# Two-layer graph network: score and bias rows spread by TensorE, first loads reordered, weight parts and one adjT later

## The chip, the cores and the metric

The kernel runs on one core of one Trainium2 chip. The metric is the time of one execution on the device in microseconds (us), the median of several runs. Lower is better.

## What is computed

128 graphs of 128 nodes with 256 features pass through two residual blocks, each on a layer-normed and rectified input:

```python
h = relu(layernorm(x))                       # block 1
Xw = h @ Wv + bv;  sj = Xw @ aw[:d, 0];  si = Xw @ aw[d:, 0]
e = leaky_relu(sj[:, None, :] + si[:, :, None] + ab[0], 0.2)
T = adj * exp(e);  T = T / (T.sum(-1) + 1e-12)
x = x + relu(h @ Wk[0] + bk[0] + T @ h @ Wk[1] + bk[1] + T @ T @ h @ Wk[2] + bk[2])
h = relu(layernorm(x))                       # block 2
y = relu(adj @ (h @ W1) + b1);  y = relu(adj @ (y @ W2) + b2)
out = x + adj @ (y @ W3) + b3
```

## The kernel before

The graphs go in 64 pairs (`G = 2`). A fully unrolled loop of 67 rounds (`rounds`, L215) writes the program of every engine; in round i four pairs are in flight: pair a = i (layer norm, scores, attention), b = i - 1 (end of block 1, second layer norm, first product with adj), c = i - 2 (GCN layers 1 and 2), d = i - 3 (last product, output, store). The order on each engine is written out by hand in the function `one` of that engine, and semaphores join the engines; an engine takes its instructions strictly in that order. Most products are made of three: each operand is cut into a high part (ScalarE copies it to fp32r) and a low part (VectorE or GpSimd subtracts), and high x high, high x low and low x high are summed in PSUM. The names end in `_hi` and `_lo`.

Round 0 and the code ahead of it hold the set-up. **SP** (L276 to L294) issues the loads of x and adj blocks of the first pairs; `aw_bc`, `bv_bc`, `ab_bc` (score vector and its biases), `bk_bc` and `bias_out` are loads that read one row and write it to all 128 partitions (256, 128, 0.5, 384 and two of 128 KB). **ScalarE's** queue issues Wv and the three Wk. **VectorE** forms `wva` = Wv times each half of aw by four `dot`s (L771) and `half_c` from bv, aw and ab (`score_constant`). The score columns are two more columns of the weight `w_p2`, so that `p2_product` also gives the scores; `scores_copy` (L431) takes them as `uv`, and `spread_scores` (L871) spreads them over partitions. **GpSimd** makes the low parts of the Wk (L365 to L368), then in round 0 `sum_biases` (L370) which waits for all loads counted by `biases_in`, `adjT_low`, and `gcn_weights_low` (the low parts of W1, W2, W3). `adjT_hi`, `adjT_lo` are parts of the transposed adj that only the last product `z3_product` reads. **TensorE** has transposes of the identity that nothing reads (`keep_busy`, L1009): 19 before the first work, 18 after `turn_h` of pair 0, 19 in round 1, and some in the last rounds.

The chain of a pair through block 1: `x_statistics`, `rstd` (GpSimd), `x_norm` -> `turn_h` (transposed h in `bank_turned`) -> `hT_high`, `hT_low` -> `p2_product`, `p01_product` -> `attention` (`alpha`), `aT_high`, `aT_low` -> `ap_product` -> `y1_sum` (`y_full`), `y1_high`, `y1_low` -> `ay_product` -> `h_sum` (`hb`) -> `residual` (`x1`) -> `x1_statistics`, `rstd`, `shift`, `norm` (`h`) -> `m_product` -> `m_high`, `m_low` -> `z1_product` -> `layer_result(0)` (`y__hi`, `y_full`) -> `y_low(0)` -> `s2_product`. `p0_bias` (L694) adds the summed block-1 bias, and `out_bias` (L337) on GpSimd makes x1b = x1 + b3, which `finish` reads two rounds later.

Of the kernel before, what the change touches and what calls it, by code (L numbers as in the profile page):

```python
# [38 lines left out]
BUSY_BEFORE, BUSY_BETWEEN, BUSY_SECOND, BUSY_TAIL = 19, 18, 19, 16  # L39
# [8 lines left out]
def gnn_kernel(nc, x, adj, Wv, bv, aw, ab, Wk, bk, W1, b1, W2, b2, W3, b3, out):  # L48
    N_PAIRS = x.shape[0] // G
    ctx = ExitStack()  # L50
    with ctx:
# [25 lines left out]
        bk_bc = sb("bk_bc", [P, K, D])  # L77
# [170 lines left out]
        def _(sp):  # L248
# [35 lines left out]
            sp.dma_start(bk_bc[:], bk.rearrange("(o k) d -> o k d", o=1).to_broadcast([P, K, D]))\  # L284
              .then_inc(biases_in, 16)
            load_adj_blocks(1, 1)
            for g in range(G):
                sp.dma_start(bias_out[:, g, :], row(b3).to_broadcast([P, D])).then_inc(biases_in, 16)
# [20 lines left out]
        def _(pool):  # L309
            pool.memset(ident[:], 0.0).then_inc(ident_zero, 1)  # L310
# [69 lines left out]
            def one(i, k):  # L380
# [697 lines left out]
```

## Time and profile before

| | us |
|---|---|
| median of 3 runs (881.37 to 883.54) | 881.63 |
| the profiled execution's own time | 881.72 |
| its span, first to last instruction | 879.9 |
| PE busy in the span | 864.7 |
| VectorE busy | 760.2 |
| ScalarE busy | 628.2 |
| GpSimd busy | 435.8 |

In rows of the profile PE is TensorE, PEld its weight loads, DVE VectorE, ACT ScalarE, POOL GpSimd, SP SyncE. A row of the timeline gives start and duration, engine, line, operation, output<-inputs, count, and in brackets how long the engine was idle before it and what released it. Digits behind tile names are left out there, so `y_full` and `stats` stand for several tiles. Two engines' durations overlap freely; the time of the program is that of the chain through them.

### The profile page before, as it was taken

How to read it: one execution, taken by the hardware profiler on the slowest of the kernel's cores; microseconds unless marked ns; L12 is line 12 of the kernel's file. 1: busy time of each engine (PE TensorE's matmuls, PEld its weight loads, DVE VectorE, ACT ScalarE, POOL GpSimd, SP SyncE). 2: the span in 40 equal slices, each digit the busy share in tenths (PEclk: the TensorE clock that was granted, in tenths of full speed). 3: DMA queues.
4: the chain of work that ended last, by engine and by line, in shares of the span. 5: the costliest groups of instructions: out<-in, count | busy, mean ns of one | idle time of the engine just before them, and what ended most of it. 6: DMA issues, size and time to landing. Idle time of an engine off the chain costs nothing.

```text
span 879.9 us, 20848 instructions
## 1 busy us (share of the span) xinstructions
PE 864.7 (98%) x6480; PEld 817.7 (93%) x6480; DVE 760.2 (86%) x2001; ACT 628.2 (71%) x1543; POOL 435.8 (50%) x532
## 2 busy tenths in 40 slices
PE   8899999999999999999999999999999999999996
PEld 7799999999999999999999999999999999999996
DVE  5789889889889889889889889899889889889872
ACT  4477777777777777777777777777777777777773
POOL 4454454454454454454454454454454454454452
PEclk9899999999999999999999999999999999999999
DMA  8112122122122122122122122122122122122001
GB/s 202 36 34 57 36 61 56 36 61 56 37 61 57 35 61 56 36 61 57 36 61 58 35 61 57 35 62 56 35 61 57 35 62 57 35 61 58 18 25 37
DMA packets 107869, 46.18 MB, mean 52 GB/s; under 512 B 72560, under 2 KB 107504, under 8 KB 107760
## 3 DMA queue, kind: packets, MB, share of 16 engines
q1 hardware_dynamic: 106672, 43.81, 20.0%
q8 instruction: 53, 0.87, 0.4%
q10 hardware_dynamic: 1088, 1.05, 0.4%
q14 instruction: 56, 0.46, 0.2%
HBM read 28.05 MB, written 16.78 MB: 51 GB/s over the span
## 4 chain that ended last, share of the span: by engine, by line
PE 95%; SPq 1%; POOL 1%; ACT 1%; issue 1%; DMA 1%; DVE 0%; DVEq 0%; ACTq 0%; POOLq 0%
PE bank L856 43%; PE bank_p L856 35%; PE bank_turned L856 7%; PE bank_T L856 5%; PE bank_turned L867 3%; PE bank_T L877 2%; SPq L261 1%; DMA bias_col<-in_L_gnn_b 1%; POOL w_gcn_lo L361 0%; PE bank_p L1012 0%; POOL bias_h L377 0%; ACT h L487 0%; ACT y_full L524 0%; DVE aT_lo L573 0%; SPq L252 0%
## 5 line engine op out<-in xcount | busy, mean ns | idle before, releaser
L334 POOL TENSOR_TENSOR y__lo<-y_full,y__hi 128x256 fp32r<-128x256 f32 x256 | 190.1, 764 | 112.3 <-ACT y_full L524 112.3
L325 POOL TENSOR_TENSOR rstd<-veps,minus_half 128x2 f32<-128x2 f32 x128 | 88.9, 695 | 236.4 <-DVE veps L596 236.4
L856 PE MATMUL bank_p<-w_p_hi,h0T_hi 128*128 128x258 f32 (+1 forms) x512 | 176.3, 360 | 0.1
L856 PE MATMUL bank_p<-w_p_lo,h0T_hi 128*128 128x258 f32 (+1 forms) x512 | 165.3, 339 | 0.0
L856 PE MATMUL bank_p<-w_p_hi,h0T_lo 128*128 128x258 f32 (+1 forms) x512 | 142.1, 339 | 0.7 <-DVE h0T_lo L629 0.7
L856 PE MATMUL bank<-w_gcn_hi,y__hi 128*128 128x256 f32 x512 | 132.8, 292 | 1.5 <-ACT y__hi L524 1.3
L856 PE MATMUL bank<-w_gcn_lo,y__hi 128*128 128x256 f32 x512 | 127.8, 282 | 0.0
L524 ACT ACTIVATE y__hi<-bank,bias_col 128x256 fp32r<-128x256 f32 x256 | 119.7, 467 | 3.0 <-PE bank L856 3.0
L524 ACT ACTIVATE y_full<-bank,bias_col 128x256 f32<-128x256 f32 x256 | 121.6, 475 | 0.0
L350 POOL TENSOR_TENSOR adjT_lo<-adjT_full,adjT_hi 128x256 fp32r<-128x256 f32 x64 | 64.9, 1015 | 82.8 <-ACT adjT_hi L429 82.8
L856 PEld LDWEIGHTS bank_p<-w_p_hi,h0T_hi 128*128 128x128 f32 x512 | 97.3, 190 | 6.2 <-POOL w_p_lo L356 0.3
L856 PEld LDWEIGHTS bank_p<-w_p_lo,h0T_hi 128*128 128x128 f32 x512 | 97.1, 190 | 5.5
L856 PEld LDWEIGHTS bank<-w_gcn_hi,y__hi 128*128 128x128 f32 x512 | 97.4, 190 | 2.1 <-ACT y__hi L524 1.5
L856 PEld LDWEIGHTS bank<-w_gcn_lo,y__hi 128*128 128x128 f32 x512 | 97.5, 190 | 0.0
L856 PEld LDWEIGHTS bank_p<-w_p_hi,h0T_lo 128*128 128x128 f32 x512 | 83.4, 188 | 12.3 <-DVE h0T_lo L629 0.9
L344 POOL TENSOR_TENSOR x1b<-x,bias_out 128x512 f32<-128x512 f32 x64 | 82.9, 1296 | 0.0
L856 PE MATMUL bank<-w_gcn_hi,y__lo 128*128 128x256 f32 x512 | 82.2, 283 | 0.0
L487 ACT ACTIVATE h<-x,nshift,rstd 128x256 f32<-128x256 f32 x128 | 69.9, 593 | 15.5 <-DVE nshift L619 15.5
L573 DVE TENSOR_TENSOR s_lo<-bank,s_hi 128x512 fp32r<-128x512 f32 x64 | 44.3, 692 | 41.4 <-ACT s_hi L507 41.4
L453 ACT ACTIVATE z<-bank_T,uv 128x128 f32<-128x128 f32 x128 | 40.0, 364 | 55.8 <-PE bank_T L877 55.7
L507 ACT ACTIVATE s_hi<-bank 128x512 fp32r<-128x512 f32 x64 | 38.2, 597 | 53.4 <-PE bank L856 53.4
L856 PEld LDWEIGHTS bank<-adjT_full,s 128*128 128x128 f32 x512 | 66.8, 191 | 6.2 <-ACT s L501 1.1
(92 smaller groups left out, 2346.2 us busy)
## 6 DMA issues: line engine op xcount, KB each, us to landing
x_in<-in_x SPq DMA_DIRECT2D x64, 256.0 KB, 3.0
x_new<-x_out SPq DMA_DIRECT2D x64, 256.0 KB, 2.2
adj_blocks<-in_adj SPq DMA_DIRECT2D x256, 32.0 KB, 2.3
w_raw<-in_L_gnn_Wk ACTq DMA_DIRECT2D x3, 256.0 KB, 6.9
w_raw<-in_L_gnn_W SPq DMA_DIRECT2D x3, 256.0 KB, 5.5
bk_bc<-in_L_gnn_bk SPq DMA_DIRECT2D x1, 384.0 KB, 6.1
wv_raw<-in_L_gnn_Wv ACTq DMA_DIRECT2D x1, 256.0 KB, 3.8
aw_bc<-in_L_gnn_aw SPq DMA_DIRECT2D x1, 256.0 KB, 5.6
```

The costliest lines, as they stand in the source:

```text
L325: pool.tensor_tensor(rstd[n][k % 2][:], veps[n][k % 2][:], minus_half[:], ALU.pow)\
L334: pool.tensor_tensor(y[n][1][:, c], y_full[n][:, c], plain(y[n][0][:, c]), ALU.subtract)\
L344: pool.tensor_tensor(x1b[k][:], x1[k % 2][:], bias_out[:], ALU.add).then_inc(x1b_made, 1)
L350: pool.tensor_tensor(adjT[k][1][:], adjT_full[k][:], plain(adjT[k][0][:]), ALU.subtract)\
L453: last = act.activation(z[k % 2][:, g, :], spread_ps[:, g, :], ACT.Prelu, bias=uv[k % 2][:, g, 0:1], alpha=SLOPE)
L487: last = act.activation(h1[k % 2][:, g, :], x1[k % 2][:, g, :], ACT.Relu, bias=nshift[k % 2][:, g:g + 1], scale=rstd[1][k % 2][:, g:g + 1])
L507: act.activation(s3[0][:], s3_ps, ACT.Copy).then_inc(s3_hi, 1)
L524: act.activation(dst[:, c], (z1_ps, z2_ps)[n][:, c], ACT.Relu, bias=bias_col[n][:, c:c + 1]).then_inc(made, 1)
L573: dve.tensor_tensor(dst, src, plain(hi), ALU.subtract).then_inc(signal, 1)
L856: return pe.matmul(dst, stationary, moving, start=start, stop=stop, skip_group_check=True)
L867: last = pe.transpose(turned_ps[:, c, g, :], n0[k % 2][:, g, c * P:(c + 1) * P], ident[:])
L877: last = pe.transpose(spread_ps[:, g, :], uv[k % 2][:, g, 1:2].to_broadcast([P, P]), ident[:])
```

## The change

Rows of aw and bv (2 KB, 1 KB) are loaded into one partition, and a product with a column of ones, in fp32, spreads each over 128 partitions in PSUM, from where ScalarE copies them to `aw_bc` and `bv_bc`. The three rows of bk and the row of b3 are loaded the same way; one product of ones with the three rows both sums and spreads them (`bias_h`), another spreads b3 (`bias_out`). Both biases now exist once and are read for both graphs through an access pattern of step 0. `sum_biases` is gone. On SP the bias rows come before adj of pair 1, x of pair 2 before W2 and W3, W1 after adj of pair 1. GpSimd makes the low part of W1 alone in round 0, those of W2 and W3 in round 1, and adjT_low of pair 0 in round 1; `out_bias` moves from pair b to pair c. ScalarE makes the high parts of W2, W3 late in round 1, and adjT_hi of pair 0 there too. TensorE has 11, 7 and 8 `keep_busy` in place of 19 and 18; the 19 of round 1 are gone, and `p2_product` of pair 1 stands ahead of `ay_product` of pair 0. On VectorE `hT_low` of pair 1 stands ahead of `y1_low` of pair 0.

```diff
-BUSY_BEFORE, BUSY_BETWEEN, BUSY_SECOND, BUSY_TAIL = 19, 18, 19, 16
+BUSY_FIRST, BUSY_BEFORE, BUSY_BETWEEN, BUSY_TAIL = 11, 7, 8, 16
...
             load_x(0, 0)
-            sp.dma_start(aw_bc[:], aw.rearrange("(h d) o -> o h d", h=2).to_broadcast([P, 2, D]))\
-              .then_inc(score_weights_in, 16)
-            sp.dma_start(bv_bc[:], row(bv).to_broadcast([P, D])).then_inc(score_consts_in, 16)
+            sp.dma_start(aw_row[:], aw.rearrange("(o d) x -> o (d x)", o=1)).then_inc(score_rows_in, 16)
+            sp.dma_start(bv_row[:], row(bv)).then_inc(score_rows_in, 16)
             sp.dma_start(ab_bc[:], row(ab).to_broadcast([P, 1])).then_inc(score_consts_in, 16)
             load_x(1, 1)
             load_adj_blocks(0, 0)
+            sp.dma_start(bk_rows[:], bk).then_inc(bias_rows_in, 16)
+            sp.dma_start(b3_row[:], row(b3)).then_inc(bias_rows_in, 16)
+            load_adj_blocks(1, 1)
             sp.dma_start(w_raw[:, K], W1.rearrange("(c p) d -> p c d", p=P)).then_inc(gcn_weights_in[0], 16)
...
+            load_x(2, 2)
             for n, w in ((1, W2), (2, W3)):
...
 # GpSimd, one(i, k)
-                if first(i):
-                    sum_biases()
                 if c is not None:
                     y_low(1, c, k - LAG_C)
-                if b is not None:
-                    out_bias(b, (k - LAG_B) % ROUND)
-                if (n := here(i, 0)) is not None:
+                    out_bias(c, (k - LAG_C) % ROUND)
+                if first(i):
+                    gcn_weights_low((0,))
+                if second(i):
+                    gcn_weights_low((1, 2))
+                    adjT_low(0, 0)
+                if (n := here(i, 0)) is not None and not first(i):
                     adjT_low(n, k)
-                if first(i):
-                    gcn_weights_low()
...
+            def rows_copied():
+                act.wait_ge(score_rows_spread, 2)
+                act.activation(aw_bc[:].rearrange("p h d -> p (h d)"), bank_2[:], ACT.Copy).then_inc(score_rows_copied, 1)
+                act.activation(bv_bc[:], bank_T[:, 0:D], ACT.Copy).then_inc(score_rows_copied, 1)
+
+            def biases_copied():
+                act.wait_ge(bias_rows_spread, 2)
+                act.activation(bias_h[:], bank_3[:, 0:D], ACT.Copy).then_inc(bias_rows_copied, 1)
+                act.activation(bias_out[:], bank_3[:, D:2 * D], ACT.Copy).then_inc(bias_rows_copied, 1)
+
+            rows_copied()
             act.wait_ge(p2_weights_in, 16)
...
                 if first(i):
                     p01_weights_high()
+                    biases_copied()
                 if second(i):
-                    gcn_weights_high()
+                    y1_high(0, 0)
+                    gcn_weights_high((0,))
...
+                if second(i):
+                    gcn_weights_high((1,))
+                if a is not None and not first(i):
                     y1_high(a, k)
+                if second(i):
+                    gcn_weights_high((2,))
+                    adjT_high(0, 0)
+                if a is not None and not first(i):
                     adjT_high(a, k)
...
                 y1_sum(0, 0)
+                hT_low(1, 1)
                 y1_low(0, 0)
...
             pe.wait_ge(ident_made, 1)
+            keep_busy(BUSY_FIRST)
+            pe.wait_ge(row_ones_made, 1)
+            pe.wait_ge(score_rows_in, 16 * 2)
+            matmul(bank_2[:], ones[0:1, :], aw_row[:], True, True).then_inc(score_rows_spread, 1)
+            matmul(bank_T[:, 0:D], ones[0:1, :], bv_row[:], True, True).then_inc(score_rows_spread, 1)
             keep_busy(BUSY_BEFORE)
...
                 if second(i):
-                    keep_busy(BUSY_SECOND)
+                    p2_product(a, k)
...
+                if first(i):
+                    pe.wait_ge(bias_rows_in, 16 * 2)
+                    matmul(bank_3[:, 0:D], ones[:], bk_rows[:], True, True).then_inc(bias_rows_spread, 1)
+                    matmul(bank_3[:, D:2 * D], ones[0:1, :], b3_row[:], True, True).then_inc(bias_rows_spread, 1)
```

The start of TensorE's program (`bank<-ident` or `bank_p<-ident` is `keep_busy`), before:

```order
L849 UNCONDITIONAL_BRANCH
L1012 MATMUL bank<-ident 128x128 x19
L867 MATMUL bank_turned<-ident,n_0 128x128 x4
L1012 MATMUL bank<-ident 128x128 x18
L856 MATMUL bank_p<-w_p_hi,h0T_hi 128x258
```

and with the change:

```order
L1035 MATMUL bank_p<-ident 128x128 x11
L875 MATMUL bank<-aw_row,ones 128x512
L875 MATMUL bank_T<-bv_row,ones 128x256
L1035 MATMUL bank_p<-ident 128x128 x7
L886 MATMUL bank_turned<-ident,n_0 128x128 x4
L1035 MATMUL bank_p<-ident 128x128 x8
L875 MATMUL bank_p<-w_p_hi,h0T_hi 128x258
```

Two products stand in the queue between the first and the second group of unread transposes, and behind a wait for two loads. Further on, between `p2_product` and `spread_scores` of pair 0, stand the two bias products:

```order
L875 MATMUL bank_p<-w_p_lo,h0T_hi 128x258
L875 MATMUL bank_p<-w_p_hi,h0T_lo 128x258 x4
L875 MATMUL bank<-bk_rows,ones 128x256
L875 MATMUL bank<-b_row,ones 128x256
L898 MATMUL bank_T<-ident,uv 128x128 x2
```

TensorE at the turn from round 0 to round 1, before and with the change (`n_1` is pair 1's normed input, `y_0` pair 0's y1):

```order
L867 MATMUL bank_turned<-ident,n_1 128x128 x4
L1012 MATMUL bank<-ident 128x128 x19
L856 MATMUL bank_T<-y_0_hi,aT_hi 128x256
L856 MATMUL bank_T<-y_0_lo,aT_hi 128x256
L856 MATMUL bank_T<-y_0_hi,aT_lo 128x256
```

```order
L886 MATMUL bank_turned<-ident,n_1 128x128 x4
L875 MATMUL bank_p<-w_p_hi,h0T_hi 128x258
L875 MATMUL bank_p<-w_p_lo,h0T_hi 128x258
...
L875 MATMUL bank_p<-w_p_hi,h0T_lo 128x258 x4
L875 MATMUL bank_T<-y_0_hi,aT_hi 128x256
L875 MATMUL bank_T<-y_0_lo,aT_hi 128x256
L875 MATMUL bank_T<-y_0_hi,aT_lo 128x256
```

The 19 transposes are gone, and pair 1's first product stands where they stood, ahead of pair 0's `ay_product` (`bank_T<-y_0`). GpSimd after the weight parts of the Wk, before and with the change:

```order
L325 TENSOR_TENSOR rstd_1<-veps_1,minus_half 128x2
L373 TENSOR_TENSOR bias_part<-bk_bc 128x256
L377 TENSOR_TENSOR bias_h<-bias_part,bk_bc 128x256 x2
L350 TENSOR_TENSOR adjT_lo<-adjT_full,adjT_hi 128x256
L361 TENSOR_TENSOR w_gcn_lo<-w_raw,w_gcn_hi 128x512 x3
L325 TENSOR_TENSOR rstd_0<-veps_0,minus_half 128x2 x2
L344 TENSOR_TENSOR x1b<-x_0,bias_out 128x512
L350 TENSOR_TENSOR adjT_lo<-adjT_full,adjT_hi 128x256
```

```order
L333 TENSOR_TENSOR rstd_1<-veps_1,minus_half 128x2
L369 TENSOR_TENSOR w_gcn_lo<-w_raw,w_gcn_hi 128x512
L333 TENSOR_TENSOR rstd_0<-veps_0,minus_half 128x2 x2
L369 TENSOR_TENSOR w_gcn_lo<-w_raw,w_gcn_hi 128x512 x2
L358 TENSOR_TENSOR adjT_lo<-adjT_full,adjT_hi 128x256 x2
L342 TENSOR_TENSOR y__lo<-y_full,y__hi 128x256 x2
```

The bias sums are gone, x1b is no longer between `rstd` and `adjT_lo`, and the low parts of W2, W3 and of both pairs' adjT now stand directly ahead of pair 0's first `y__lo`.

## Rows read from the trace of the kernel before

**Rows 1.** The page, part 2: granted clock in tenths, 40 slices
```profile
PEclk9899999999999999999999999999999999999999
```

**Rows 2.** Waits of PE after 38 us: who for whom, total, times, longest
```profile
PE bank L856 <- DVE s_lo L573: 1.4, 1, 1.4
...
PE bank_p L856 <- ACT aT_hi L467: 0.2, 1, 0.2
```

**Rows 3.** Stretches: length, PE, PEld, DVE, ACT, POOL busy, clock, DMA, GB/s
```profile
31.00:38.00 7.00, 6.31 (x30) 6.02 (x31) 4.08 (x11) 1.84 (x4) 1.01 (x1) 0.52 0.00 0
```

**Rows 4.** Timeline, `spread_scores` of pair 2
```profile
41.29 0.38 PE L877 MATMUL bank_T<-ident,uv 128*128 128x128 f32 x2
```

**Rows 5.** DMA issues up to 13 us, median us to landing
```profile
aw_bc<-in_L_gnn_aw SPq DMA_DIRECT2D x1, 256.0 KB, 5.6
...
ab_bc<-in_L_gnn_ab SPq DMA_DIRECT2D x1, 0.5 KB, 7.7
```

**Rows 6.** Timeline, pair 0's way to its products: start, us, engine, operation
```profile
1.52 4.31 PE L1012 MATMUL bank<-ident 128*128 128x128 f32 x19 [1.52 <-POOL ident L316]
...
4.24 0.75 DVE L579 BATCH_NORM_STATS2 stats<-x_in 128x6 f32<-128x256 f32 x2 [4.24 <-DMA x_in<-in_x]
...
7.03 0.42 DVE L750 CUSTOM_DVE_ANT_0 scratch<-wv_raw,aw_bc 128x256 f32<-128x256 f32 x1
...
7.50 0.63 ACT L410 ACTIVATE w_p_hi<-w_raw 128x512 fp32r<-128x512 f32 x1 [3.40 <-DMA w_raw<-in_L_gnn_Wk]
...
8.08 3.46 PE L1012 MATMUL bank<-ident 128*128 128x128 f32 x18
...
11.30 0.36 PE L856 MATMUL bank_p<-w_p_hi,h0T_hi 128*128 128x258 f32 x1
...
13.03 0.26 ACT L439 ACTIVATE uv<-bank_p,half_c 128x4 f32<-128x4 f32 x1 [1.28 <-PE bank_p L856]
...
13.35 0.43 PE L877 MATMUL bank_T<-ident,uv 128*128 128x128 f32 x2 [0.35 <-ACT uv L439]
...
13.89 0.51 PE L856 MATMUL bank_p<-w_p_hi,h0T_hi 128*128 128x512 f32 x1
```

**Rows 7.** Timeline, one fp32 product of four matmuls at the full clock
```profile
46.33 1.05 PE L856 MATMUL bank_turned<-adjT_full,h 128*128 128x128 f32 x8
```

**Rows 8.** Timeline, aT_lo of pair 0, then from y1 of pair 0 to its h
```profile
16.32 0.43 DVE L573 TENSOR_TENSOR aT_lo<-alpha,aT_hi 128x256 fp32r<-128x256 f32 x1 [0.54 <-ACT aT_hi L467]
...
17.94 2.24 PE L1012 MATMUL bank<-ident 128*128 128x128 f32 x19
...
18.08 0.88 DVE L683 SCALAR_TENSOR_TENSOR y_full<-bank_p,rinv,p 128x256 f32<-128x256 f32 x2
...
21.21 0.69 DVE L701 TENSOR_TENSOR p0b<-bank_p,bias_h 128x512 f32<-128x512 f32 x1 [0.70 <-POOL bias_h L377]
...
23.07 0.86 DVE L710 SCALAR_TENSOR_TENSOR hb<-bank_T,rinv,p0b 128x256 f32<-128x256 f32 x2
```

**Rows 9.** Timeline, low parts of W1 to W3, then pair 1's attention
```profile
21.77 4.21 POOL L361 TENSOR_TENSOR w_gcn_lo<-w_raw,w_gcn_hi 128x512 fp32r<-128x512 f32 x3
...
29.27 1.27 POOL L344 TENSOR_TENSOR x1b<-x,bias_out 128x512 f32<-128x512 f32 x1
29.31 1.51 DVE L573 TENSOR_TENSOR aT_lo<-alpha,aT_hi 128x256 fp32r<-128x256 f32 x1 [0.77 <-ACT aT_hi L467]
29.33 0.51 PE L856 MATMUL bank_p<-p_hi,aT_hi 128*128 128x258 f32 x2 [1.84 <-ACT aT_hi L467]
...
31.22 1.85 PE L856 MATMUL bank_turned<-adjT_full,h 128*128 128x128 f32 x8
...
34.61 1.01 POOL L350 TENSOR_TENSOR adjT_lo<-adjT_full,adjT_hi 128x256 fp32r<-128x256 f32 x1 [4.07 <-ACT adjT_hi L429]
```

**Rows 10.** Chain of waits, twelve matmuls twice: start, us, what
```profile
33.76 2.93 PE bank L856 x12
...
53.58 1.43 PE bank L856 x12
```

More of the change, by code:

```diff
@@ L76, in gnn_kernel @@
         ab_bc = sb("ab_bc", [P, 1])
-        bk_bc = sb("bk_bc", [P, K, D])
+        aw_row = sb("aw_row", [1, 2 * D])
+        bv_row = sb("bv_row", [1, D])
+        bk_rows = sb("bk_rows", [K, D])
+        b3_row = sb("b3_row", [1, D])
+        ones = sb("ones", [K, P])
         scratch = sb("scratch", [P, 6, D])
@@ L240, in landed, with each_graph @@
             return (i - k) * (16 // ROUND) + 16
-        BIAS_LOADS = 1 + G + 2
+        def each_graph(row):
+            return row.rearrange("p (o d) -> p o d", o=1).to_broadcast([P, G, D])
         block = ctx.enter_context(nc.Block())
@@ L282, in _ @@
             load_adj_blocks(0, 0)
+            sp.dma_start(bk_rows[:], bk).then_inc(bias_rows_in, 16)
+            sp.dma_start(b3_row[:], row(b3)).then_inc(bias_rows_in, 16)
+            load_adj_blocks(1, 1)
             sp.dma_start(w_raw[:, K], W1.rearrange("(c p) d -> p c d", p=P)).then_inc(gcn_weights_in[0], 16)
[L284 to L288, printed above, removed]
             for n, b in enumerate((b1, b2)):
                 sp.dma_start(bias_col[n][:], b.rearrange("(c p) -> p c", p=P),
-                             allow_slow_non_contiguous=True).then_inc(biases_in, 16)
+                             allow_slow_non_contiguous=True).then_inc(columns_in, 16)
+            load_x(2, 2)
             for n, w in ((1, W2), (2, W3)):
@@ L297, in one @@
                 if (n := here(i, -2)) is not None:
-                    load_x(n, (k + 2) % ROUND)
+                    if not first(i):
+                        load_x(n, (k + 2) % ROUND)
                     load_adj_blocks(n, (k + 2) % ROUND)
@@ L356, in k_weights_low, with gcn_weights_low @@
                 pool.tensor_tensor(lo, w_raw[:, n], plain(hi), ALU.subtract).then_inc(signal, 1)
-            def gcn_weights_low():
-                for n in range(K):
+            def gcn_weights_low(layers):
+                for n in layers:
                     pool.wait_ge(gcn_weights_hi, n + 1)
@@ L368, in _ @@
                 k_weights_low(2 + n, n, w_p01[0][:, :, cols], w_p01[1][:, :, cols], p01_weights_cut)
-            def sum_biases():
-                pool.wait_ge(biases_in, 16 * BIAS_LOADS)
-                pool.tensor_tensor(bias_part[:], bk_bc[:, 0, :], bk_bc[:, 1, :], ALU.add)\
-                    .then_inc(bias_h_made, 1)
-                pool.wait_ge(bias_h_made, 1)
-                for g in range(G):
-                    pool.tensor_tensor(bias_h[:, g, :], bias_part[:], bk_bc[:, 2, :], ALU.add)\
-                        .then_inc(bias_h_made, 1)
             def one(i, k):
@@ L507, in s3_high, with gcn_weights_high @@
                 act.activation(s3[0][:], s3_ps, ACT.Copy).then_inc(s3_hi, 1)
-            def gcn_weights_high():
-                for n in range(K):
+            def gcn_weights_high(layers):
+                for n in layers:
                     act.wait_ge(gcn_weights_in[n], 16)
@@ L769, in _ @@
             x_norm(0, 0)
-            dve.wait_ge(score_weights_in, 16 * 2)
+            dve.wait_ge(score_weights_in, 16)
+            dve.wait_ge(score_rows_copied, 2)
             for c in range(C):
@@ L805, in one @@
                     s3_low(d)
-                if a is not None:
+                if a is not None and not second(i):
                     hT_low(a, k)
@@ L1029, in one @@
                     ay_product(b, kb)
-                if a is not None:
+                if a is not None and not second(i):
                     p2_product(a, k)
```

32 lines of the change are left out of this document (19 added, 13 removed).

## The prediction

> **What bounds the kernel now.** I read the page first: PE is busy for 864.7 of 879.9 us, and the granted clock is full but for one slice near the start, from 22 to 44 us [rows 1]. Next the waits of PE after 38 us: only some 4 us in five waits, all but 0.2 us of it in the last rounds [rows 2]. So from round 2 on PE works without a stop, every round costs the sum of its products, and the change adds and removes no product there. It can only move the point at which this unbroken stretch begins. Then the windows: from 31 to 38 us PE has a granted clock of 0.52, so it ran there at the lower of its levels, 1.2 GHz, in place of 2.4 [rows 3]. All the rest is read in the timeline of the first 42 us. The landmark of the sum is `spread_scores` of pair 2, at 41.29 us [rows 4]; behind it PE has no wait but the 0.2 us.
>
> **Step 1: the front.** Before, the loads that write one row to 128 partitions land 5.6 and 7.7 us after issue [rows 5], and x of pair 0 is there at 4.24 us [rows 6]. The rows of aw and bv are issued behind that x, at the old places of `aw_bc` and `bv_bc` (the load of 0.5 KB took 7.7 us, queued behind both). No row shows a one-partition load. Bounds: with x at 4.24, or with the 7.7 us of `ab_bc`, at 9.4. I take 4.3, since nothing but x stands ahead of them now.
>
> The Trainium skill, "DMA: Bandwidth & Descriptors", section "Latency and other measured facts", gives tiny transfers about 0.8 us as a floor; by it the rows would be there before the 11 transposes end, and the sum below would gain another 0.3 us. The 0.5 KB load at 7.7 us speaks for the queue instead.
>
> Products: four fp32 matmuls of 128 columns take 0.8 us at the full clock (0.2 each; 1.05 with the drain) [rows 7]. The transposes show which clock the front has: 19 in 4.31 us at the start, 0.23 each [rows 6], against 19 in 2.24 us in round 1, 0.12 each [rows 8]. The front is at half speed (though the clock row shows nothing of it [rows 1]). So aw (512 columns) costs 1.6 us and bv 0.8: they end at 6.7. ScalarE copies both in about 1.1 us (0.63 for 512 columns [rows 6]), to 7.8. The first `dot` comes at 7.8 in place of 7.03, the high part of Wk[2] at 7.8 in place of 7.50. PE: 7 transposes to 8.3, `turn_h` 0.9, 8 transposes 1.8: `p2_product` at 11.0, before 11.30, where it waited for the end of the 18 transposes and not for its weights. A gain of 0.3 that the sum gives back at once: behind `p2_product` stand the two bias products of 256 columns, 0.8 us at the full clock, and ScalarE copies both (0.4 each) ahead of `scores_copy`. Before, `p2_product` took from 11.30 to 13.03 with its drain. Now it is done at 12.7, the bias products at 13.4, the copies at 14.2, so `uv` starts at 14.2 in place of 13.03. `spread_scores` follows 0.32 us later, `p01_product` 0.2 after that, 14.7 in place of 13.89, where it had waited for GpSimd's weight parts. **Front: 0.8 us later.** Bounds: 0 (the full clock comes early, all products halve) to 1.2 (b3's row, issued near 8 us, lands 5.6 us later, at 13.6, when the queue needs it at 12.7). I take 0.7.
>
> **Step 2: round 1 up to h.** Before, VectorE went from y1 of pair 0 (18.08, ready at 18.96) to `hb` at 23.07: 4.1 us [rows 8]. In it were 0.70 us until the bias sum came from GpSimd, a wait of the same length for the high part of y1, and five instructions. With the change the bias stands ready, and `hT_low` of pair 1 fills the wait for y1's high part, since `turn_h` and ScalarE's copy of pair 1 are done by then. What is left is `hT_low`, `y1_low`, `p0_bias` and the statistics of pair 2, about 0.69 each: 2.75. **Gain 1.35.** The 19 transposes cost nothing before (PE waited behind them for `y1_low`), and give nothing now. `p2_product` of pair 1 takes their place and is done at about 20.8, ready long before VectorE is. It no longer matters.
>
> **Step 3: attention of pair 1.** `aT_lo` took 1.51 us, from 29.31, while GpSimd's x1b ran from 29.27 for 1.27 [rows 9]; that of pair 0 took 0.43 with nothing beside it [rows 8]. x1b is moved a round later, to where its pair's x1 is long made. `aT_lo` ended at 30.82, and PE's last two attention products waited for it. All six take 0.8 in one piece from 29.33, to 30.1; `m_product` could start there in place of 31.22. **Gain 1.1**, and 0.15 from `residual`, which no longer runs beside GpSimd's W2 and W3 parts. `m_product` of pair 0 so starts 2.6 us earlier, less step 1.
>
> **Step 4: m to the scores of pair 2.** Before 31.22 to 41.29, 10.1 us. Most of it was at half clock: twelve matmuls of 256 columns took 2.93 us at 33.76 and 1.43 at 53.58 [rows 10]; `m_product`, z1, `turn_h` and `ay` together cost 3.4 us over the full clock. At full clock the waits come out: m 0.8, ScalarE's copy 0.7, z1's high part 1.0, a wait of 0.5 for `m_low`, z1's rest 0.4, `turn_h` 0.4, `ay` 0.9 with its wait, 0.2 for `hT_high` (ScalarE now has W2's, W3's and pair 0's adj parts ahead of it, 1.6 us), `p2` 1.5, s2's high part 0.9, 0.7 for `y_low`, s2's rest 0.5: 8.5. The `y_low` wait is what the change itself adds. GpSimd had two of three parts of 4.21 us (21.77 on) early; now W2, W3, adjT 0 and adjT 1 (1.27, 1.27, 1.01, 1.01) [rows 9] stand directly ahead of pair 0's `y_low`. **Gain 1.6.** Bounds: 0 if the clock falls again, 2.3 without the GpSimd queue.
>
> Against this step speaks the Trainium skill, "SBUF — State Buffer", section "Who interferes with whom": a VectorE instruction with two SBUF inputs and a GpSimd one that reads SBUF block each other in turn. This is what `aT_lo` shows, and by it the moved parts may do to `y1_low` and `residual` of pair 1 what x1b did; the sum would then be 1.1 us worse, the price of `aT_lo` once.
>
> **Sum.** 1.35 + 1.1 + 0.15 + 1.6 + 0.15 (most of PE's 0.2 in round 2) = 4.35, less 0.7: 3.6 us. Loads of W and x have slack: 1 MB less is moved. The tail's x1b of the last pair comes while its last layer is at work. Both cost 0. The profiled execution had 881.72 us, 0.09 above the median. So 881.7 - 3.6 = 878.1; I say **878.2**.
>
> **Rivals.**
> - **The clock falls again.** It fell about 31.3 us, after PE had waited 1.84 and 0.80 us with 0.7 of work between [rows 9]. The second gap goes, but the first becomes 2.2 (round 1 is paced by VectorE still), and the transposes of round 1 are gone, so gaps of about 1 us come ahead of it. Then step 4 gives nothing and the queues on GpSimd are hidden: gain 2.7 - 0.7 = 2.0, **879.7**. Beside it: the Trainium skill, "TensorE: Matmul & The Clock Gate", section "HAM oscillation", blames long single waits; by that the clock would stay up.
> - **GpSimd's queue becomes the wait.** If the four parts are blocked by VectorE's two-input work, or come late because ScalarE's high parts do, s2's rest waits 1.2 us more: **879.4**. For it: they stand in a row, and ScalarE makes W3's only after y1. Against: 64 pairs show adjT_lo at 1.01 us.
> - **The score rows come late: slower.** PE, ScalarE and VectorE all stand in order behind them. If they land at 9.4 as by `ab_bc`'s 7.7 us, the `dot`s start at 12.9; with 1.7 for them and the two small instructions behind, `p2_product` starts at 14.6, 3.3 late, and `p01_product`, with the bias products and copies, 4.3. PE idles for 5 us ahead of it, the clock stays down, and steps 2 to 4 give 2.7: 881.7 + 4.3 - 2.7, **883.3.** With the clock down it decides from rows landing some 2.3 us late, at 6.6.
> - **The change doesn't do what it says:** the blocking is moved, not removed. W1's low part (1.27) now meets `y1_low` of pair 0, at 1.2, and step 3 gives 0.2 in place of 1.1: 3.6 - 1.2 - 0.9, 1.5 gained, **880.2**.
>
> **How the numbers follow.** What this kernel's measurement can tell from no change is 0.3%, 2.6 us; faster by that is below 879.0. Forecast 0.50 (its own range 877.0 to 879.0), clock 0.22, GpSimd 0.13, score rows 0.07, ineffective 0.08. Of the forecast nearly all is below 879.0, of clock and GpSimd together a quarter: faster 0.57. Slower by over 2.6 us needs the rows later still: 0.04. Same: 0.39. The range: below, a front at no cost and no GpSimd wait, 881.7 - 5.0 = 876.7; above, up to the ineffective case and a little of the front's bound, 881.0.
>
> **What would show it.** Right: `p2_product` of pair 0 near 11.0, `uv` near 14.2, `hb` near 22.4, `aT_lo` of pair 1 at 0.43, `m_product` near 29.3, granted clock 1.00 from 31 to 38, `spread_scores` of pair 2 near 37.8, the round at the same 13.2 us. Wrong: PE's wait for a row load over 1 us, a clock of 0.5 after 28 us, `y__lo` of pair 0 behind adjT_lo by more than 1 us, or any new wait of PE after round 3.

## The result, and the profile after

| | before | changed |
|---|---|---|
| median, us | 881.94 (881.37 to 884.11, 17 runs) | 881.07 (879.08 to 881.72, 16 runs) |
| ratio, 95% interval | | 0.9983 [0.9975, 0.999] |
| the profiled execution, its span | 881.72, 879.9 | 879.17, 877.4 |

One changed execution of 1708.92 us, far outside the rest, is left out here, as are three below (936.29, 1905.07 and 2176.69 us). The gain is 0.9 us where 3.5 was forecast: within 0.3%, and just above the top of the range (881.0).

The times of the changed kernel are two groups, by the mean granted clock of each run: four runs at 879.1 to 879.2 with 0.999, twelve at 881.0 to 881.7 with 0.994 to 0.997. The kernel before has them too: in the later comparisons 879.0 to 880.1 in 12 of its 112 runs (0.996 to 0.999), and 880.7 to 884.2 in the rest. In 43 of the 112 the mean clock was 0.992 or 0.993 (median 883.0); none of the 27 timed runs of the changed kernel, later ones included, was that low. The profile below is of the upper clock, that of [rows 3] of the lower. **At the upper clock (0.998 or more) the two kernels are 0 to 0.3 us apart.** The two profiled executions differ by 2.6 us and the medians by 0.9, so the profiles flatter the change by 1.7 us, and the experiments have to take the clock apart from the rest.

The windows of the changed kernel (columns as in [rows 3]) show the full clock where the kernel before had 0.52:

```profile
31.00:38.00 7.00, 6.01 (x48) 5.45 (x46) 6.77 (x13) 5.57 (x13) 5.21 (x5) 1.00 0.00 0
```

The timeline of its front, against [rows 6]:

```profile
4.29 0.75 DVE L596 BATCH_NORM_STATS2 stats<-x_in 128x6 f32<-128x256 f32 x2 [4.29 <-DMA x_in<-in_x]
5.08 2.04 PE L875 MATMUL bank<-aw_row,ones 1*128 1x512 f32 x2 [0.82 <-DMA bv_row<-in_L_gnn_bv]
6.92 1.06 PE L875 MATMUL bank_T<-bv_row,ones 1*128 1x256 f32 x2
8.01 0.60 ACT L409 ACTIVATE aw_bc<-bank 128x512 f32<-128x512 f32 x1 [3.89 <-PE bank_T L875]
9.04 0.42 DVE L767 CUSTOM_DVE_ANT_0 scratch<-wv_raw,aw_bc 128x256 f32<-128x256 f32 x1 [1.88 <-ACT bv_bc L410]
9.48 1.37 POOL L364 TENSOR_TENSOR w_p_lo<-w_raw,w_p_hi 128x512 fp32r<-128x512 f32 x1 [3.08 <-ACT w_p_hi L419]
9.74 1.40 DVE L767 CUSTOM_DVE_ANT_0 scratch<-wv_raw,aw_bc 128x256 f32<-128x256 f32 x1
11.74 2.72 POOL L364 TENSOR_TENSOR w_p_lo<-w_raw,w_p_hi 128x512 fp32r<-128x512 f32 x2 [0.89 <-ACT w_p_hi L424]
12.04 0.36 PE L875 MATMUL bank_p<-w_p_hi,h0T_hi 128*128 128x258 f32 x1 [0.20 <-DVE w_p_lo L590]
12.41 0.92 DVE L767 CUSTOM_DVE_ANT_0 scratch<-bv_bc,aw_bc 128x256 f32<-128x256 f32 x1
13.26 1.49 DVE L767 CUSTOM_DVE_ANT_0 scratch<-bv_bc,aw_bc 128x256 f32<-128x256 f32 x1
15.18 0.15 DVE L780 TENSOR_SCALAR half_c<-c_sum 128x1 f32<-128x1 f32 x1
15.43 0.26 ACT L448 ACTIVATE uv<-bank_p,half_c 128x4 f32<-128x4 f32 x1
15.75 0.43 PE L898 MATMUL bank_T<-ident,uv 128*128 128x128 f32 x2 [0.97 <-ACT uv L448]
```

The rows landed 0.8 us behind x, the two products, at half speed, took 2.9 us, and three of six `dot`s took 0.92 to 1.49 us in place of 0.42: those that ran beside GpSimd's `w_p_lo`. `half_c` came at 15.18 and `uv` right behind it, 2.4 us later than before.

The timeline of rounds 1 and 2, against [rows 8, 9]:

```profile
20.10 0.88 DVE L700 SCALAR_TENSOR_TENSOR y_full<-bank_p,rinv,p 128x256 f32<-128x256 f32 x2
23.57 0.88 DVE L727 SCALAR_TENSOR_TENSOR hb<-bank_T,rinv,p0b 128x256 f32<-128x256 f32 x2
29.65 0.43 DVE L590 TENSOR_TENSOR aT_lo<-alpha,aT_hi 128x256 fp32r<-128x256 f32 x1 [0.77 <-ACT aT_hi L476]
29.67 0.51 PE L875 MATMUL bank_p<-p_hi,aT_hi 128*128 128x258 f32 x2 [1.91 <-ACT aT_hi L476]
30.51 1.05 PE L875 MATMUL bank_turned<-adjT_full,h 128*128 128x128 f32 x8
32.79 3.00 POOL L369 TENSOR_TENSOR w_gcn_lo<-w_raw,w_gcn_hi 128x512 fp32r<-128x512 f32 x2 [3.14 <-ACT w_gcn_hi L521]
33.27 1.37 DVE L590 TENSOR_TENSOR y_lo<-y_full,y_hi 128x512 fp32r<-128x512 f32 x1 [0.16 <-ACT y_hi L488]
35.74 1.43 POOL L358 TENSOR_TENSOR adjT_lo<-adjT_full,adjT_hi 128x256 fp32r<-128x256 f32 x2
37.14 1.86 POOL L342 TENSOR_TENSOR y__lo<-y_full,y__hi 128x256 fp32r<-128x256 f32 x2
39.63 0.38 PE L898 MATMUL bank_T<-ident,uv 128*128 128x128 f32 x2
```

From y1 to hb 3.47 us (before 4.99), from hb to `m_product` 6.94 (8.15), from there (30.51) to `spread_scores` of pair 2 9.12 (10.07). The landmark so came 1.7 us earlier, and the end of the program 2.5: another 0.4 us was gained in the very next round (13.1 us to the scores of pair 3, before 13.6), the rest in small pieces later. The view of PE's waits behind 38 us has a new one, in place of the 0.2 of [rows 2]:

```profile
PE bank L875 <- POOL y__lo L342: 1.0, 1, 1.0
```

### The profile page after: what moved, and what is told of

Its sections match the earlier page's. It is cut to its first block, busy times and chain, and to the rows that moved or that the text cites. A ratio compares the mean times of both kernels' runs of the same rounds, so it can differ in the third digit from the quotient of the medians.

```text
span 877.4 us, 20808 instructions
## 1 busy us (share of the span) xinstructions
PE 861.0 (98%) x6458; PEld 812.2 (93%) x6458; DVE 761.1 (87%) x2001; ACT 629.4 (72%) x1547; POOL 433.5 (49%) x530
## 4 chain that ended last, share of the span: by engine, by line
PE 96%; ACT 1%; POOL 1%; DVE 1%; issue 1%; DMA 0%; SPq 0%; DVEq 0%; POOLq 0%
PE bank L875 43%; PE bank_p L875 36%; PE bank_turned L875 7%; PE bank_T L875 5%; PE bank_turned L886 3%; PE bank_T L898 2%; POOL w_gcn_lo L369 0%; DMA bv_row<-in_L_gnn_bv 0%; PE bank_p L1035 0%; DVE scratch L767 0%; POOL y__lo L342 0%; POOL rstd L333 0%; POOL adjT_lo L358 0%; ACT y_full L533 0%; ACT h L496 0%
```

## Experiments

Three explanations stood against each other. **Front:** the score rows and the slowed `dot`s eat the gain. **GpSimd:** the moved low parts block `y_lo` of pair 1 and delay `y__lo`. **Clock:** the gain of step 4 was the clock's, and it falls in most runs with the change as well. Fastest runs are given beside the medians, since they stand for the upper clock; those of the changed kernel are 879.1 here and 879.3 when it was timed again, so 0.2 to 0.4 us between jobs means nothing.

### One edit alone, and repairs made singly

The kernel before with x1b alone moved (GpSimd, `one`):

```diff
                     y_low(1, c, k - LAG_C)
-                if b is not None:
-                    out_bias(b, (k - LAG_B) % ROUND)
+                    out_bias(c, (k - LAG_C) % ROUND)
```

> The kernel before with one edit: x1b is made for pair c in place of pair b. Theory A (step 3 holds: blocking of aT_lo by GpSimd's x1b cost 1.1 us on PE's path): aT_lo of pair 1 takes 0.43 in place of 1.51, m_product of pair 0 starts 0.7 to 1.1 us earlier (30.1 to 30.5 in place of 31.2), and the median falls by 0.5 to 1.5 us. Rival (the blocking only moves): aT_lo stays over 1 us or another VectorE instruction of round 1 grows by 1 us; no change of the median within 0.3 us.

Measured: 878.49 (877.68 to 880.68), ratio 0.9967 [0.9956, 0.9978]. `aT_lo` takes 0.43 and `m_product` starts at 30.59. One moved instruction gains more than the whole change; the rest of the change must cost. Six of its twelve runs are at 877.7 to 878.0. The median fell by 3.3 us where 0.5 to 1.5 was expected, so more than the moved block is in it.

The changed kernel with the bias products behind `turn_h` of pair 1, and ScalarE's copies behind y1:

```diff
                 if second(i):
+                    pe.wait_ge(bias_rows_in, 16 * 2)
+                    matmul(bank_3[:, 0:D], ones[:], bk_rows[:], True, True).then_inc(bias_rows_spread, 1)
+                    matmul(bank_3[:, D:2 * D], ones[0:1, :], b3_row[:], True, True).then_inc(bias_rows_spread, 1)
                     p2_product(a, k)
...
```

> The changed kernel with the two bias products moved from between p2_product and spread_scores of pair 0 to behind turn_h of pair 1, where PE waited 0.70 us, and ScalarE's two copies to behind y1_high of pair 0. Theory F (the front's price is mostly these: in the changed kernel p2_product began at 12.04 and uv at 15.43, 3.4 us, where before it took 1.7): uv of pair 0 comes 1.0 to 1.6 us earlier, at 13.8 to 14.4, and so does all behind it; median 1.0 to 1.6 us below the changed kernel. Rival G (half_c, late because its dots are blocked by GpSimd's low parts, holds uv at 15.3 by itself): uv at 15.2 to 15.4 and no gain above 0.2 us.

Measured: 880.61 (879.19 to 881.07), ratio 0.9981. `uv` is at 15.58, right behind `half_c` at 15.32: in the queue of PE and ScalarE the bias products were in nobody's way. The fastest runs are those of the changed kernel, 879.2.

The changed kernel with 16 unread transposes where PE waits for `aT_hi` of pair 1:

```diff
                     p01_product(a, k, 1, (1,))
+                    if second(i):
+                        pe.wait_ge(bias_rows_copied, 2)
+                        keep_busy(16, bank_3[:, 0:P])
                     ap_product(a, k)
```

> The changed kernel with 16 unread transposes (1.7 us at the full clock) in PE's wait of 1.9 us ahead of ap_product of pair 1. Theory C (the two groups of times of the changed kernel, near 879.1 and 881.1, differ by whether TensorE's granted clock falls near 30 us behind that wait): nearly all runs near 879.1 to 879.4, granted clock of the program 0.999 in all of them, median 1.5 to 2 us below the changed kernel's. Rival (the groups come from elsewhere, the loads or the front): the two groups stay, median within 0.4 us of the changed kernel's or slightly later, since the transposes may hold ap_product by 0.1 us.

Measured: 879.14 (878.93 to 881.43), ratio 0.9975. Seven of eleven runs at 878.9 to 879.2, four at 880.7 to 881.4 with a clock of 0.996 to 0.997. The wait for `aT_hi` shrinks from 1.91 to 0.16. More runs keep the clock, but not all.

The changed kernel with GpSimd's part of W3 and both adjT_lo behind `y_low(0)` of round 2:

```diff
+                if i == 2:
+                    gcn_weights_low((2,))
+                    adjT_low(0, 0)
+                    adjT_low(1, 1)
...
-                    gcn_weights_low((1, 2))
-                    adjT_low(0, 0)
...
+                    gcn_weights_low((1,))
```

> The changed kernel with GpSimd's low part of W3 and both adjT_low moved behind y_low and the two rstd of round 2. Theory Q (GpSimd's queue holds the second half of s2_product by 0.98 us): y__lo of pair 0 is done by 37.2 in place of 39.0, PE's wait of 0.98 goes, spread_scores of pair 2 at 38.6 to 38.8 in place of 39.63, and the median falls by 0.6 to 1.0 us. Rival (the wait only moves: s3_product or z3_product now wait for the late parts, or rstd of pair 1 for them): PE waits 0.5 us or more in round 2 or 3 elsewhere, median within 0.3 us of the changed kernel's.

Measured: 880.29 (879.71 to 882.03), ratio 0.9987; its fastest runs 0.6 above the changed kernel's. `spread_scores` of pair 2 came at 38.44, 1.2 us earlier, but PE then waited 1.6 us for `y__lo` behind it: the queue is as long, only its place differs.

### The front

The second experiment's edit, and the score rows by the old loads to all partitions:

```diff
-            sp.dma_start(aw_row[:], aw.rearrange("(o d) x -> o (d x)", o=1)).then_inc(score_rows_in, 16)
-            sp.dma_start(bv_row[:], row(bv)).then_inc(score_rows_in, 16)
+            sp.dma_start(aw_bc[:], aw.rearrange("(h d) o -> o h d", h=2).to_broadcast([P, 2, D]))\
+              .then_inc(score_rows_in, 16)
+            sp.dma_start(bv_bc[:], row(bv).to_broadcast([P, D])).then_inc(score_consts_in, 16)
...
```

> The changed kernel with the score rows loaded by the broadcasts of before (11 and 8, then 18 transposes, as before) and the bias products behind turn_h of pair 1. Theory D (the front's 2 us come from the score rows' way over PE and ScalarE: it puts VectorE's six dots beside GpSimd's low parts of the Wk, which block them): the dots take 0.42 each again and start near 7.0, uv of pair 0 is at 12.9 to 13.2 in place of 15.4, y_full of pair 0 near 18.1 in place of 20.1, hb near 21.6, and the fastest runs (clock 0.999) come to 877.0 to 877.6, 1.6 to 2.1 us below the changed kernel's 879.1. Rival (the front is off the path, since round 1 has slack on VectorE): fastest runs within 0.5 us of 879.1.

Measured: 879.88 (878.83 to 880.21), ratio 0.9966 [0.9952, 0.9979]. `uv` at 12.36, but `p01_product` only at 14.56: it waited 1.47 us for `w_p_lo`, and that for Wk, whose three loads took 7.3 us to land, in place of 6.0 in the changed kernel. And in this profile the clock fell in the front, 0.69 from 16 to 20 us. The fastest run, 878.83, is within the rival's 0.5 us of 879.1: of the 2 us next to nothing is regained by this alone.

```profile
14.56 0.50 PE L875 MATMUL bank_p<-w_p_hi,h0T_hi 128*128 128x512 f32 x1 [1.47 <-POOL w_p_lo L365]
```

The changed kernel with the `dot`s reading the score vector in PSUM, where the product left it, and the bias products later:

```diff
-                    dot(wva[:, c, h:h + 1], wv_raw[:, c, :], aw_bc[:, h, :], 2 * c + h, wva_made)
+                    dot(wva[:, c, h:h + 1], wv_raw[:, c, :], bank_2[:, h * D:(h + 1) * D], 2 * c + h, wva_made)
...
```

> The changed kernel with the dots reading the spread aw straight from PSUM (no copy of aw by ScalarE; bv is still copied), so that a dot has one input in SBUF at most besides bv's, and with the bias products behind turn_h of pair 1. Theory D: all six dots take about 0.42 although GpSimd's low parts run beside them, half_c is there before 13.5 in place of 15.3, uv of pair 0 at 13.5 to 13.9, and the fastest runs come to 877.4 to 878.0. Rival (the dots are slow for another reason than two inputs in SBUF beside GpSimd): some dots still take 0.9 to 1.5 us, uv stays at 15 or later.

Measured: 880.07 (879.45 to 880.87), ratio 0.9971 [0.9962, 0.9979], six runs at 879.5 to 879.6 and six at 880.6 to 880.9. VectorE's timeline:

```profile
11.83 0.41 DVE L766 CUSTOM_DVE_ANT_0 scratch<-bv_bc,bank 128x256 f32<-128x256 f32 x1
12.16 0.42 DVE L766 CUSTOM_DVE_ANT_0 scratch<-bv_bc,bank 128x256 f32<-128x256 f32 x1
12.62 0.46 DVE L776 TENSOR_TENSOR c_sum<-bva 128x1 f32<-128x1 f32 x1
13.12 1.21 DVE L778 TENSOR_TENSOR c_sum<-c_sum,ab_bc 128x1 f32<-128x1 f32 x1
14.36 0.15 DVE L780 TENSOR_SCALAR half_c<-c_sum 128x1 f32<-128x1 f32 x1
```

The `dot`s are free of GpSimd now. But the block goes to the next VectorE instruction with two inputs in SBUF, a sum of one element per partition: 1.21 us, for 0.16 in the changed kernel. So `uv` comes 0.8 us earlier, at 14.61, and not the 2.5 that the three `dot`s had lost. Nor does the 0.8 show in the time: the fastest runs are no faster than the changed kernel's 879.1, where 877.4 to 878.0 was expected.

### The weight parts, and the clock in the front

The changed kernel with the parts of W2 and W3 at their old places on ScalarE and GpSimd:

```diff
-                    gcn_weights_low((0,))
+                    gcn_weights_low((0, 1, 2))
...
-                    gcn_weights_high((0,))
+                    gcn_weights_high((0, 1, 2))
```

> The changed kernel with both parts of W2 and W3 made where they were before (ScalarE at the start of round 1, GpSimd at the end of round 0); adjT of pair 0 stays late. Theory W (moving these parts costs 0.98 us of PE's wait for y__lo of pair 0 and makes y1_low of pair 1 1.37 us long in place of 0.68): y_lo of pair 1 takes 0.68, PE waits under 0.3 us for y__lo in round 2, spread_scores of pair 2 at 38.3 to 38.8 in place of 39.63, fastest runs 878.1 to 878.5. Rival (the same work in front of uv of pair 1 and beside residual delays round 1 by as much): hb and x1 of pair 0 0.5 us later, fastest runs within 0.3 us of 879.1.

Measured: 880.92 (879.01 to 882.78), ratio 0.9974 [0.9962, 0.9986]. `y_lo` of pair 1 takes 0.69 again, but the clock is at 0.5 just there, and the median tells nothing of it. The fastest runs, 879.0 to 879.1, are the changed kernel's, as the rival said. So each of the three repairs (`dot`s, bias products, W parts) gains nothing that shows by itself.

x1b moved, and the 16 transposes, on the kernel before:

> The kernel before with x1b for pair c and 16 unread transposes ahead of ap_product of pair 1. Theory C (the clock falls behind PE's wait of 1.9 us there and costs 0.2 to 3 us, differently from run to run): runs lie within 0.6 us of one another, all with clock 0.998 or more, median 877.2 to 877.9 against 878.5 for the same kernel without them. Rival: the spread from 877.7 to 880.7 stays, because the clock falls for another wait (in the front or round 1's start).

Measured: 879.42 (878.45 to 880.42), ratio 0.9964 [0.9949, 0.9978]. In the profile the clock is full from 24 to 50 us, and fell in the front, where PE had waited 0.80 and 1.47 us:

```profile
12.00:16.00 4.00, 1.92 (x7) 1.44 (x8) 2.35 (x8) 2.08 (x6) 3.15 (x3) 0.92 0.70 131
16.00:20.00 4.00, 4.00 (x17) 3.32 (x16) 1.18 (x4) 1.08 (x3) 1.51 (x3) 0.65 0.85 222
```

There are two places to lose the clock, and a cover at one leaves the other. The front of this kernel is that of the kernel before, so the place in the front was there before the change.

### Four kernels side by side

x1b moved, and of the change only the reorder of round 1:

```diff
+                hT_low(1, 1)
                 y1_low(0, 0)
...
-                    keep_busy(BUSY_SECOND)
+                    p2_product(a, k)
```

> The kernel before with x1b moved, and with the reorder of round 1 alone: hT_low of pair 1 ahead of y1_low, p2_product of pair 1 in place of the 19 transposes; loads, bias sum and weight parts as before. Theory (the reorder is a gain of its own, and the rest of the change gives it back): hb of pair 0 some 0.7 us earlier than 23.1, since the sum of biases on GpSimd still ends at 21.2; fastest runs near 877.0, median about 0.7 below that of x1b moved alone. Rival (the reorder takes PE's cover away and the clock falls more often): fastest runs the same 877.7 or lower, but median at or above that of x1b moved alone.

The changed kernel again:

> The changed kernel again, beside the others on one chip. If the earlier runs are typical: a quarter of the runs near 879.1 with clock 0.999, the rest near 881.2; median 0.8 us below the kernel before. If the chip made the difference, the median is 3 us below.

On the changed kernel four repairs at once: `dot`s from PSUM, bias products later, W parts at their old places, 16 transposes:

> The whole change with four repairs: dots read the score rows in PSUM, bias products behind turn_h of pair 1, parts of W2 and W3 at their old places, 16 unread transposes ahead of ap_product of pair 1. If the losses are the ones named (front held by half_c and slow dots 0.8 us, y_low and y__lo blocked 0.7 us, clock), they add: uv at 14.6, y_low of pair 1 at 0.69 us, no wait for y__lo, clock full, median 877.5. Rival (each only moves the wait, as when they were made alone): median 879.5 or more, no better than x1b moved alone.

x1b moved alone, again:

> The kernel before with x1b moved and nothing else, again, on the chip of the other three. If one move is worth more than the whole change: median 2 to 3 us below that of the changed kernel in this job, fastest runs 877.7 against 879.1. If the earlier difference was chance of the clock: medians within 0.8 us of each other.

| | median | runs | ratio to before (882.1) |
|---|---|---|---|
| x1b and reorder | 879.99 | 879.66 to 882.93, 11 | 0.9984 [0.9973, 0.9994] |
| changed | 880.36 | 879.27 to 881.88, 11 | 0.9981 [0.9971, 0.999] |
| repaired | 878.44 | 878.24 to 878.52, 5 | 0.9956 [0.9944, 0.9969] |
| x1b alone | 879.33 | 878.08 to 880.79, 7 | 0.9971 [0.9957, 0.9985] |

The reorder alone is a loss, not 0.7 us of gain: its fastest runs are 1.6 us above those of x1b alone. Its profile has the lower clock in three stretches (0.63 from 16 to 20 us, 0.57 from 22 to 26, 0.58 from 32 to 36), so its times can't be split, but it shows what the expectation forgot: GpSimd's W parts start at 23.22, right when `y1_low`, now behind `hT_low`, does:

```profile
23.22 4.20 POOL L359 TENSOR_TENSOR w_gcn_lo<-w_raw,w_gcn_hi 128x512 fp32r<-128x512 f32 x3 [0.28 <-ACT w_gcn_hi L509]
23.27 1.78 DVE L570 TENSOR_TENSOR y_lo<-y_full,y_hi 128x512 fp32r<-128x512 f32 x1
```

x1b alone is again ahead of the changed kernel, by 1.0 us and not the 2 to 3 expected. The changed kernel need not lose the clock near 31 us as in [rows 3]: in the profiled run of this job (mean clock 0.996) it falls in the front, behind PE's wait of 0.90 us for `uv`, and `m_product` starts at 32.30 in place of 30.51:

```profile
12.00:16.00 4.00, 3.10 (x19) 2.39 (x17) 3.90 (x11) 1.19 (x5) 2.55 (x2) 0.99 1.05 278
16.00:20.00 4.00, 4.00 (x12) 3.25 (x13) 1.90 (x8) 2.12 (x6) 0.69 (x1) 0.58 0.21 36
```

The repaired kernel is 0.9 us above the 877.5 expected, but faster than with any one of its repairs. It has `half_c` at 14.22, `y_lo` of pair 1 at 0.69, and the landmark where the prediction had put it, 37.8:

```profile
32.90 0.69 DVE L585 TENSOR_TENSOR y_lo<-y_full,y_hi 128x512 fp32r<-128x512 f32 x1
35.52 1.47 POOL L342 TENSOR_TENSOR y__lo<-y_full,y__hi 128x256 fp32r<-128x256 f32 x2 [0.64 <-ACT y_full L531]
37.82 0.38 PE L894 MATMUL bank_T<-ident,uv 128*128 128x128 f32 x2
```

### Taking the repairs apart

> The repaired kernel without the 16 unread transposes in the gap ahead of ap_product of pair 1. If the clock is most of what is missing: its fastest runs are at 878.2 to 878.5 as those of the repaired kernel, but half or more of its runs lie 1.5 to 2.5 us above, at a mean clock of 0.997 or lower, median 879.5 or more. If the parts and the front did it: all runs at 878.5, as with the transposes.

> The repaired kernel again: dots in PSUM, bias products later, parts of W2 and W3 early, 16 transposes in the gap. If the cover holds the clock: no run above 879.0, median 878.4. If the first five runs were luck: a third or more near 880.5.

> The repaired kernel but with the parts of W2 and W3 where the change put them. If GpSimd's queue costs 0.7 to 1.0 us (y_low of pair 1 at 1.37, y__lo at 1.86 and waited for): median 879.2, spread_scores of pair 2 near 38.7 in place of 37.8. If it is hidden: 878.4.

The fourth leaves the score rows to the old loads, and covers the wait behind them:

```diff
                     spread_scores(a, k)
+                    if first(i):
+                        keep_busy(10, bank_3[:, 0:P])
```

> The repaired kernel with the score rows by the old loads to all partitions, and 10 more unread transposes behind spread_scores of pair 0, where PE waits 1.5 us for GpSimd's low parts. If spreading by TensorE is worth less than it costs (uv at 12.4, p01_product held to 14.6 by the late Wk loads, against 15.2): median 877.9, 0.5 below the repaired kernel. Rival (the loads of 384 KB push Wk back and the low parts come later still): 878.8 or more.

| | median | runs | mean clock of the runs |
|---|---|---|---|
| repaired | 878.35 | 878.23 to 878.38, 5 | 0.999 to 1.0 |
| without the 16 transposes | 879.75 | 878.24 to 880.92, 8 | 0.999 in three, 0.995 to 0.997 in five |
| W2, W3 parts late | 879.15 | 878.8 to 879.2, 5 | 0.998 to 1.0 |
| score rows by loads, both covers | 877.59 | 877.28 to 877.69, 5 | 0.999 to 1.0 |

All four medians as the first theory of each said, to within 0.3 us. No profile shows where the third had its landmark, expected near 38.7. **The clock:** without the cover the fastest runs are the same 878.2, five of eight lie 1.5 to 2.7 us above, and in the profile, behind a wait of PE of 2.25 us, the granted clock is 0.50 from 32 to 36 us, the lower level, 1.2 GHz. A matmul of 256 columns follows the last at 0.21 us there, and not at 0.12:

```profile
29.50 0.50 PE L871 MATMUL bank_p<-p_hi,aT_hi 128*128 128x258 f32 x2 [2.25 <-ACT aT_hi L474]
...
32.97 0.41 PE L871 MATMUL bank<-m_hi,w_gcn_lo 128*128 128x256 f32 x1
33.18 0.41 PE L871 MATMUL bank<-m_hi,w_gcn_hi 128*128 128x256 f32 x1
```

**GpSimd:** 0.8 us. **Score rows by TensorE** cost 0.8 us against the loads they replace (the second cover came with them, but both kernels had the full clock in all runs); the last is the fastest kernel of the study, 0.9951 [0.9939, 0.9963] of the kernel before, 4.3 us.

Last, how much of that belongs to the change at all. The kernel before with x1b moved and both covers, and with the covers alone:

> The kernel before with x1b moved, 16 unread transposes ahead of ap_product of pair 1 and 10 behind spread_scores of pair 0. If the clock is the main cost and x1b the main edit: all runs within 0.5 us of each other, median 878.0, so that the bias rows, the reorder and the loads are worth 0.4 us together (877.6 with them). If the rest of the change is worth its step 2: 878.9 or more.

> The kernel before with the two covers and nothing of the change. If the clock alone accounts for the gap between its runs of 879.3 and of 882: all runs at 879.0 to 879.5, median 879.3, 2.6 us below the kernel before. If x1b's collision is what lets the clock fall (PE waits for aT_lo behind the first wait): half the runs still at 881 or more.

Measured beside a kernel before of 882.22: 878.00 (877.91 to 879.46, 7 runs), ratio 0.9955 [0.9939, 0.9971], and 879.25 (878.91 to 879.7, 11 runs), ratio 0.9971 [0.996, 0.9982]. 26 instructions that compute nothing gain 3.0 us; x1b adds 1.25; all the rest of the change, in its best form, 0.4 (from two jobs, so not resolved).

One thing here is not the clock's. The profiled execution of the first of the two is its slowest run, 879.46 with the clock at 0.999, 1.1 us above the next. In it Wk landed a little earlier, GpSimd began 0.1 us ahead of VectorE's two one-element sums, and these took 1.17 and 1.19 us:

```profile
11.26 2.49 POOL L354 TENSOR_TENSOR w_p_lo<-w_raw,w_p_hi 128x512 fp32r<-128x512 f32 x2 [1.90 <-ACT w_p_hi L412]
11.37 1.17 DVE L756 TENSOR_TENSOR c_sum<-bva 128x1 f32<-128x1 f32 x1
12.58 1.19 DVE L758 TENSOR_TENSOR c_sum<-c_sum,ab_bc 128x1 f32<-128x1 f32 x1
14.05 0.26 ACT L436 ACTIVATE uv<-bank_p,half_c 128x4 f32<-128x4 f32 x1 [2.35 <-DVE half_c L760]
```

In the profile of the kernel before, the second sum began at 11.27 and GpSimd at 11.30, and both sums took 0.16. So the landing of Wk is a second thing that differs from run to run; in how many runs it costs time isn't known.

## Why the prediction was wrong

**Bound: right; landmark: right to about 1 us.** The round is 13.2 us in both. But from the landmark to the end it is 838.6 us before and 837.8 with the change (837.5 to 839.6 over the other profiled runs), where the sum had put 0.15 for all that lies behind it.

**Step 1, the front: mis-sized, 2.0 us where 0.7 was put (0.8 worked out, bound 1.2).** The profiled run's `y_full` came 2.0 us later. The rows landed at 5.08 and not 4.3 (0.8). The products took 2.9 and not 2.4, with a drain each. And the term that the sum left out: it priced the `dot`s at the 0.42 of [rows 6], a `dot` with GpSimd idle beside it, and moved them into GpSimd's `w_p_lo` without a price. `half_c` became the last input of `uv`; the bias products, on which the sum spent 1.6 us, cost nothing, as the second experiment shows.

**Step 2: right**, 1.52 for 1.35, but not for the order alone. Done by itself, with the bias sum and the W parts left as they were, the reorder was a loss.

**Step 3: right**, 1.2 for 1.25, and the run with x1b alone shows it to be the one edit that pays: 1.25 us with the clock held.

**Step 4: this is where it failed.** The 1.6 us were the price of the clock in a single profiled run of before (2.3, less 0.7 for GpSimd's queue), and were booked as a gain of the change, with "the clock falls again" as a rival of 0.22. In truth the clock differs from run to run in both kernels: up in 12 of 112 runs before, in 4 of 16 and 5 of 11 runs with the change. Nothing the change does covers PE's wait of 1.9 us, and the front is a second place to lose it, in both kernels. The changed kernel's median so stands 2.0 us above its own upper group. In the run where the clock stayed up, step 4 gave 0.95 and not 1.6: it took 9.1 us where 8.5 was summed, because the moved W2 and W3 parts blocked `y_lo` (1.37 for 0.69) and `y__lo` (1.86 for 1.47), so that PE waited 0.3 us for the one and 1.0 for the other, where the sum had 0.7 for the second alone. The prediction did weigh the first of them with a rule, the Trainium skill, "SBUF — State Buffer", section "Who interferes with whom", and left it out of the sum; the trace agrees with the rule, there and at the `dot`s. The repaired kernel shows both costs by their absence: its step 4 is 7.6 us.

**Sum at equal clock:** 1.5 + 1.2 - 2.0, less the 1.5 by which step 4 is longer than the repaired kernel's, is -0.8 at the landmark. This is an estimate, since no profile shows the kernel before at the full clock through step 4; with x1b moved and the clock held its step 4 is 7.6 us too. The 0.8 behind the landmark brings it to 0, and the times say 0 to 0.3 us gained. Either way there is nothing left of 3.6. The 0.9 us of the medians are that, and a better chance of the clock.

**Rivals.** The true case was three of them at once: the clock (2 us in most runs), GpSimd's queue (0.8), and a bit of the late rows (0.8 of the front). Each was priced alone, the first two at 879.7 and 879.4, both far from 881.1; the third, with rows 5 us late, at 883.3, but they were 0.8 us late. What stays open: what decides in which runs the clock falls, since the same waits stand in profiles with and without a fall.

## What to carry to other kernels

When a profile shows a stretch at the lower clock, ask first in how many runs it does: a mean clock beside each time tells most of it (not all, as the slow run at 0.999 shows), and one profile can flatter a change by 2 us of 880. If the time is lost there, cover every wait ahead of the stretch with work that nobody reads, and do it before anything else is moved; it cost nothing here and was worth more than the whole change. A VectorE instruction that is moved must be priced beside what GpSimd does at its new time: in these runs one with two inputs in SBUF, even one element wide, waited GpSimd's instruction out, and an operand left in PSUM freed it only until the next such instruction. And where two repairs stand one behind the other on the way, each alone may show nothing: the three here gained only together, 1.0 us between the fastest runs of one job (878.2 against 879.3).

## What the runs showed of the hardware

- A sum of one element per partition took 1.21 us beside GpSimd's `w_p_lo`, and 0.16 without. Two inputs in SBUF are not needed for it: a copy of four elements per partition, with one input, took 1.02 us beside `w_p_lo` in the kernel before, and 0.17 with GpSimd idle in the changed kernel.

```profile
8.53 1.02 DVE L775 CAST w_p_hi<-wva 128x4 fp32r<-128x4 f32 x1
```

- The clock fell in the front of the changed kernel (0.58 from 16 to 20 us) behind a wait of 0.90 us, the longest since PE's first instruction 0.92, and in the same profile not behind the later wait of 1.90 us. In its other profile it fell behind neither 0.97 nor 1.91 us. The Trainium skill, "TensorE: Matmul & The Clock Gate", section "HAM oscillation", blames long single waits; these runs speak against it as the only cause.
- Rows of 2 and 1 KB, issued right behind the 256 KB of x, were in 3.4 us after the issue of the second, 0.8 us after x. The 0.8 us that the Trainium skill, "DMA: Bandwidth & Descriptors", section "Latency and other measured facts", gives for tiny transfers is a floor, and these rows stayed far above it.
